# Second attention of a macaron block: scores from row tiles, and the order of a group's phases

## The reference

```python
def _L1_attn_ref(data, W_qkv, b_qkv, W_out, b_out):
    N, L, D_IN, H, HD, D_OUT = (4, 256, 128, 16, 64, 128)
    DIM = H * HD
    n, l = (data.shape[0], data.shape[1])
    qkv = data @ W_qkv + b_qkv
    q = qkv[:, :, :DIM].reshape(n, l, H, HD)
    k = qkv[:, :, DIM:2 * DIM].reshape(n, l, H, HD)
    v = qkv[:, :, 2 * DIM:].reshape(n, l, H, HD)
    scores = jnp.einsum('nqhd,nkhd->nhqk', q, k)
    attention = jax.nn.softmax(scores / jnp.sqrt(jnp.float32(HD)), axis=3)
    out = jnp.einsum('nhql,nlhd->nqhd', attention, v).reshape(n, l, DIM)
    return out @ W_out + b_out
```

## Time and profile before

| | |
|---|---|
| three executions | 3102.01, 3099.66, 3099.52 us; median 3099.66 |
| the profiled execution | 3094.67 us |
| its span, first to last instruction | 3092.9 us |
| mean granted TensorE clock | 0.961 of full speed |
| busy in the span | TensorE 91%, VectorE 67%, GpSimd 57%, ScalarE 56% |
| the second attention | from about 1850 to 2880 us of the span |

### The profile page before, as it was taken

One profiled execution on the slowest core, in us unless ns is written; L12 is line 12 of the kernel. 1 busy time (PEld: TensorE's weight loads), 2 busy tenths in 40 slices (PEclk: granted clock), 3 DMA queues, 4 the chain that ended last, 5 costly groups with the idle time before them and its releaser, 6 DMA issues. The chain is left out here.

```text
span 3092.9 us, 48070 instructions
## 1 busy us (share of the span) xinstructions
PE 2824.9 (91%) x16692; PEld 1889.5 (61%) x16692; DVE 2087.2 (67%) x4491; ACT 1733.2 (56%) x3334; POOL 1751.1 (57%) x1540
## 2 busy tenths in 40 slices
PE   7999999999999999989993869999999999999376
PEld 6995555555555555548882765656556565565276
DVE  5667777777677777766777437676776777767542
ACT  5665767677676767676761434444544544444033
POOL 0005989898888989881100764554554545455067
PEclk9999999999999999989995889999999999999678
DMA  3003434343343334320001436444444445443033
GB/s 99 1 15 91 102 84 103 84 96 89 85 97 91 89 86 96 85 67 11 15 22 61 94 64 137 111 94 102 110 107 103 110 95 116 92 103 90 28 78 53
DMA packets 182946, 251.89 MB, mean 81 GB/s; under 512 B 36084, under 2 KB 75569, under 8 KB 182193
## 3 DMA queue, kind: packets, MB, share of 16 engines
q1 hardware_dynamic: 168624, 238.09, 32.8%
q0 software_dynamic: 14080, 10.73, 2.5%
HBM read 31.34 MB, written 14.57 MB: 15 GB/s over the span
## 5 line engine op out<-in xcount | busy, mean ns | idle before, releaser
L1919 POOL TENSOR_TENSOR arena<-arena 128x512 f32<-128x512 f32 x1152 | 1445.0, 1282 | 675.9 <-ACT arena L1277 570.0
L1277 ACT ACTIVATE arena<-psum 128x512 f32<-128x512 f32 x1536 | 843.2, 600 | 523.4 <-PE psum L872 519.1
L1555 DVE TENSOR_REDUCE top<-psum 128x1 f32<-128x512 f32 x1536 | 958.4, 672 | 68.8 <-PE psum L872 67.8
L872 PE MATMUL psum<-stack 96*128 96x512 f32 (+3 forms) x3072 | 949.9, 431 | 19.2 <-ACT arena L1277 9.1
L872 PEld LDWEIGHTS psum<-stack 96*128 96x128 f32 (+3 forms) x3072 | 521.5, 190 | 320.5 <-issue 158.3
L923 PE MATMUL psum<-arena,values 128*32 128x512 f32 (+1 forms) x3072 | 495.9, 600 | 12.7 <-ACT arena L1277 12.7
L923 PEld LDWEIGHTS psum<-arena,values 128*32 128x32 f32 (+1 forms) x3072 | 129.7, 119 | 286.7 <-issue 228.1
L1888 POOL TENSOR_SCALAR rstd<-mv 128x4 f32<-128x4 f32 x56 | 13.1, 235 | 450.2 <-DVE mv L1417 448.9
L1586 DVE RECIPROCAL psum<-psum 128x128 f32<-128x128 f32 x256 | 243.6, 955 | 34.4 <-PE psum L955 34.4
L883 PE MATMUL psum<-halves 64*128 64x512 f32 x1536 | 214.9, 409 | 3.8 <-DVE top L1555 3.8
L757 PE MATMUL psum<-stack 128*128 128x512 f32 x768 | 211.5, 411 | 0.1
(11 more groups left out here) (176 smaller groups left out, 3528.1 us busy)
## 6 DMA issues: line engine op xcount, KB each, us to landing
stack<-halves SPq DMA_DIRECT2D x768, 128.0 KB, 2.3
stack<-halves SPq DMA_DIRECT2D x384, 256.0 KB, 4.7
tokens<-xn SPq DMA_DIRECT2D x16, 256.0 KB, 2.4
arena<-in_wg SPq DMA_DIRECT2D x16, 256.0 KB, 3.0
arena<-in_wu SPq DMA_DIRECT2D x16, 256.0 KB, 3.5
arena<-in_wd SPq DMA_DIRECT2D x16, 256.0 KB, 3.0
wqkv<-in_w_qkv SPq DMA_DIRECT2D x2, 1536.0 KB, 8.9
X<-in_x SPq DMA_DIRECT2D x8, 256.0 KB, 4.6
```

The costliest lines, as they stand in the source:

```text
L872: ins = T_.matmul(bk, st[0:k, side, slot + h, cols], st[0:k, 1 - side, slot + h, :], start=r == 0, stop=r == len(PARTS[l]) - 1)
L1277: S_.activation(prob[l][tile % N_PROB][:, h, :], psum[:, bank[key], :], ACT.Exp, scale=scale).then_inc(released[bank[key]], 1)
L1555: give(V_.reduce_max(top[i][:, column:column + 1], psum[:, bank[key], :], AX.X), key)
L1919: ins = G_.tensor_tensor(to[:, h, :], old[:, h, :], prob[l][tile % N_PROB][:, h, :], ALU.add)
```

## The change

The second attention no longer uses stacks of halves. `probabilities` takes its scores from `halves` through the same function as `maxima`: `both_heads` gets the keys and a list of rounds, three products and a fourth round of 64 rows, which multiplies rows of ones with rows of minus the maximum (`ones_rows`, `top_rows`, in the memory of the stacks; zero apart from two rows for each head). The halves are kept for four groups instead of two (`split`), in `halves` and two parts of the stacks. All copies of the halves into stacks go; the maxima are copied by four DMAs instead of two. The queries' scores of a pair are now one tile of queries of both heads, as before, but a pair is issued at a time instead of two (`AT_ONCE` goes). q, k, v and top of the second attention take their banks from the ring of the scores. `weigh` does its four tiles in `last` and none in `probs`; probabilities have eight buffers instead of five. The table of times of the second attention is new. The first attention keeps its way.

```diff
-    dict(project=(-0.11, 0.61), maxima=(0.90, 1.11), maxima2=(0.95, 1.29), rows=(1.90, 1.90), probs=(2.33, 3.28),
-         last=(3.19, 3.46), mix=(3.91, 4.52), out=(4.59, 4.83), ahead=(-2.58, -0.89), route=(4.85, 6.56),
-         ranks=(6.66, 7.31), keep=(7.88, 7.88)))
+    dict(rows=(1.82, 1.82), queries=(0.75, 0.75), keys=(0.80, 0.80), values=(1.01, 1.01), maxima=(1.04, 1.48),
+         probs=(3.03, 3.47), last=(3.43, 4.05), sums=(4.38, 4.38), mix=(4.38, 4.83), out=(4.93, 4.97),
+         ahead=(-1.52, 0.45), route=(5.03, 10.53), ranks=(9.80, 10.86), keep=(10.00, 10.00)))
...
-            self.once(self.other, (w, l, n))
+            self.once(self.products if l else self.other, (w, l, n))
...
-        self.once(self.other, ("top", l, n))
+        self.once(self.products if l else self.other, ("top", l, n))
...
+                if l == 0:
+                    self.once(self.products, ("prob", l, n, kt, h))
+                elif h == 0:
+                    for head in range(HEADS[l]):
+                        self.once(self.products, ("prob", l, n, kt, head))
+                yield
...
+        split = (halves, halves + [stack[i][:, 1, :, :] for i in range(2)])
+        top_rows = [stack[i][:, 0, 0, :] for i in range(N_STACK)]
+        ones_rows = [stack[i][:, 0, 1, 0:P] for i in range(N_STACK)]
...
-        N_PROB = 5
+        N_PROB = (5, 8)
...
+            def both_heads(keys, rounds):
+
+                banks = [place(key) for key in keys]
+                for r, (weights, moving) in enumerate(rounds):
                     for h, (bk, done) in enumerate(banks):
                         rows_h = slice(64 * h, 64 * (h + 1))
-                        ins = T_.matmul(bk, hv[rows_h, q, pair * P:(pair + 1) * P], hv[rows_h, k, :],
-                                        start=r == 0, stop=r == 2, tile_position=(64 * h, 0))
-                        if r == 2:
+                        ins = T_.matmul(bk, weights[rows_h], moving[rows_h], start=r == 0, stop=r == len(rounds) - 1,
+                                        tile_position=(64 * h, 0))
+                        if r == len(rounds) - 1:
                             ins.then_inc(done, 1)
...
+                        elif h == 0:
+                            both_heads([("prob", l, n, kt, head) for head in range(HEADS[l])],
+                                       [(hv[:, k, cols], hv[:, q, :]) for q, k in ((QH, KH), (QL, KH), (QH, KL))]
+                                       + [(ones_rows[n % N_STACK], top_rows[n % N_STACK])])
                         yield
-                    if kt == 2:
+                    if kt == 2 and l == 0:
                         weigh(l, n, 0)
                         weigh(l, n, 1)
                         yield
...
             def last_tiles(l, n):
-                weigh(l, n, 2)
-                weigh(l, n, 3)
+                for kt in range(0 if l else 2, TILES_B):
+                    weigh(l, n, kt)
                 yield
...
-                    if n >= 2:
-                        act.wait_ge(*all_stacked(l, n - 2))
-                        if l:
-                            act.wait_ge(*written(("score", l, n - 2, HEADS[l] * TILES_B - 1)))
+                    if n >= len(split[l]):
+                        act.wait_ge(*halves_used(l, n - len(split[l])))
...
             def project(l, n):
-                s, hv, st, width = n % N_STACK, halves[n % 2], stack[n % N_STACK], WIDTH[l]
+                if l:
+                    return
...
+                    if l:
+                        for h in range(HEADS[l]):
+                            Y_.dma_start(
+                                top_rows[s][64 * h + r:64 * h + r + 1, :].rearrange("a (t q) -> a t q", t=TILES_B).bitcast(fp32),
+                                part[h * TILES_B:(h + 1) * TILES_B, :].bitcast(fp32)).then_inc(max_rows[s], 16)
```

More of the change, by code:

```diff
@@ L117, in queue @@
             start, end = WHEN[l][part]
-            part = dict(ranks="route", maxima2="maxima").get(part, part)
+            part = dict(ranks="route", queries="project", keys="project", values="project").get(part, part)
             stream(part, numbers, calls, steps, at + n + start, at + n + end)
@@ L298, in last @@
     def last(self, l, n):
+        if l:
+            self.mixed.take(("o", l, n))
         yield
@@ L648, in free, with all_stacked, halves_used @@
             return (released[bank[key]], nth[key]) if nth[key] else None
[L650 to L653, removed]
+        def all_stacked(n):
+            return stacked[n % N_STACK], 16 * 3 * HEADS[0] * (n // N_STACK + 1)
+        def halves_used(l, n):
+            return written(("prob", 1, n, TILES_B - 1, HEADS[1] - 1)) if l else all_stacked(n)
         def all_max_rows(l, n):
@@ L730, in idle_tile @@
         def idle_tile(slot):
-            tile = max(t for t in range(N_GROUPS * TILES_B) if t % N_PROB == slot)
+            tile = max(t for t in range(N_GROUPS * TILES_B) if t % N_PROB[0] == slot)
             return tile_weighed(0, *divmod(tile, TILES_B)), tile_summed(0, *divmod(tile, TILES_B))
@@ L867, in project, with product @@
                 yield
[L869 to L876, removed]
-                hv = halves[n % 2]
-                banks = [place(("score", 1, n, 2 * pair + h)) for h in range(2)]
-                for r, (q, k) in enumerate(((QH, KH), (QL, KH), (QH, KL))):
+            def product(bk, st, side, h, cols, k):
+                return T_.matmul(bk, st[0:k, side, h, cols], st[0:k, 1 - side, h, :], start=True, stop=True)
+            def both_heads(keys, rounds):
+                banks = [place(key) for key in keys]
+                for r, (weights, moving) in enumerate(rounds):
                     for h, (bk, done) in enumerate(banks):
                         rows_h = slice(64 * h, 64 * (h + 1))
-                        ins = T_.matmul(bk, hv[rows_h, q, pair * P:(pair + 1) * P], hv[rows_h, k, :],
-                                        start=r == 0, stop=r == 2, tile_position=(64 * h, 0))
-                        if r == 2:
+                        ins = T_.matmul(bk, weights[rows_h], moving[rows_h], start=r == 0, stop=r == len(rounds) - 1,
+                                        tile_position=(64 * h, 0))
+                        if r == len(rounds) - 1:
                             ins.then_inc(done, 1)
@@ L901, in maxima @@
                     for i in range(HEADS[l] * TILES_B):
-                        if i % AT_ONCE == 0:
-                            for pair in range(i // 2, (i + AT_ONCE) // 2):
-                                both_heads(n, pair)
+                        qt, h = divmod(i, HEADS[l])
+                        if h == 0:
+                            cols = slice(qt * P, (qt + 1) * P)
+                            both_heads([("score", l, n, i + head) for head in range(HEADS[l])],
+                                       [(hv[:, q, cols], hv[:, k, :]) for q, k in ((QH, KH), (QL, KH), (QH, KL))])
                         yield
@@ L962, in mix @@
                     return
-                columns = [inverse[l][n % 2][:, t * P:(t + 1) * P] for t in range(TILES_B)]
+                columns = [inverse[n % 2][:, t * P:(t + 1) * P] for t in range(TILES_B)]
                 yield
```

108 lines of the change are left out of this document (59 added, 49 removed).

## The result

The changed kernel takes 3107.27 us (median of 11 runs, 3103.72 to 3112.72), the kernel before 3102.01 on the same chip (11 runs, 3098.2 to 3107.1): ratio 1.002, 95% interval 1.0011 to 1.003. So it is slower by about 5 us, just short of the 0.2% that I took as the bound of "same"; forecast was 3154, in a range from 3090 that holds the result. The profiled execution of after took 3106.33 us (span 3104.5, clock 0.960), that of before 3094.67: the profiles lie 11.6 apart, since the execution profiled of before is a quick one.

The account below looks back on a forecast made before the run. TensorE was taken to bound the kernel, busy 123.86 of 127.2 us a batch. Groups +49, seam -2, batches +12, start -7, drain +2 on 3094.67 gave 3149; 5 more for the median gave 3154, range 3090 to 3190.

Parts of the forecast that it names:

- Removing the copies: Stack copies and their DMAs in the second attention: TensorE doesn't wait for them, so removal is worth 0 by itself.
- Fewer changes of shape: TensorE's tile shapes: three changes a group instead of six, 0.21 us each, minus 0.63 us a group.
- The row tiles: Probability scores as 16 row-tile pairs instead of 16 full matmuls: 0.23 us a round, minus 0.06 us a group.
- The bank chain: Each probability pair (P) waits for a bank the previous one filled: P to P 2.0 us, plus 1.2 a group.
- Rival 1: The banks don't bind: a bank returns in 1.6 us, group 13.9 us, about 3080 in the median; chance 0.20.
- The group: One plain group of the second attention: 15.1 us against 14.3, plus 0.8 (0.81 in the sum).
- The seam: Next group's first probability pair waits for q's bank, 2.75 us after q: plus 0.24 a group, output groups excepted.
- Batch work: Normalisation, moments and router work inserted in each batch: 5 us instead of 3.3, plus 1.7 per batch.
- five such insertions: Normalisation, moments and router ranks delaying ScalarE or VectorE: about 1 us each, bounded by 0 and 1.63.
- Ends: Start and drain of the second attention's pipeline: minus 7 us at the start, plus 2 in the drain.
- Rival 2: Gain and loss cancel: P to P 1.8 us, batch waits gone, group 14.5, 3098 to 3105; chance 0.08.
- Rival 3: VectorE makes it slower still, 3200 us, if q's low half starts later than 1.9 us after q; chance 0.12.

Follow-up runs that it names:

- e5: Transposition of the maxima moved between the first two probability pairs of the next group, against the seven-bank kernel e2: 3113.96 us, ratio 1.0012.
- e9: Store of a finished batch (keep) moved from 10.00 to 10.90, behind the router's last step, against e5: 3066.14 us, ratio 0.9855.
- e7: Table of times of the kernel before (phases mixed, ten shape changes a group) put into the seven-bank kernel e2: 3141.95 us, ratio 1.0103.
- e2: Seven banks instead of five in the second attention's ring, weighed values included, against the changed kernel: 3035.87 us, ratio 0.9769 to the kernel before.

## Why the prediction was right or wrong

**Removing the copies, 0: right, as far as waits show it** (no run takes the copies away and leaves the rest). No wait for a DMA stands in TensorE's waits of the second attention, before or after, and the DMAs fell from 251.89 to 151.32 MB. In one variant a copy of the maxima was waited for, through SP's order (e5), which after doesn't have.

**Fewer changes of shape, 0.21 each: right, slightly low.** 0.24 (e5), 0.23 (e9), 0.27 (e7). The trace agrees with the rule of the Trainium skill, "TensorEngine Tiling (Array Packing)", Key Properties, that a change of tiling mode drains the array and that another tile of the same mode doesn't. Its warning, in Restrictions and Gotchas, of PSUM pressure under row tiling is what decided the case: with seven banks the change is worth -2.3%, with its five +0.2%.

**The row tiles, 0.23 a round: right,** 0.91 for four where nothing waits (e2).

**The bank chain, P to P 2.0: right, link by link;** one of the three steps is 1.94. 1.26 to the exponential, 0.60, 0.14. Rival 1 needed 1.6 and is refuted for this kernel; it describes e2.

**The group, +0.81: the sum was right in kind, measured +0.52.** Three terms were too high and one too low. P to P came to 5.94 instead of 6.0 (-0.06: one of three starts 1.94 after the last). The last P and S to the sums took 1.81 instead of 1.93 (-0.12: the last P and S ran with 0.06 less each than the links I had added up). Column phase 4.44 instead of 4.41 (+0.03). The seam took 2.61 instead of 2.75 (-0.13: ScalarE began q's high half 0.07 sooner and VectorE followed 0.07 sooner than the links I copied from other rows). Together -0.28, times 61 that is 17 us.

**Batch work, +1.7 a batch: the step that failed.** With the seam's 0.24 off for the output group that is +1.5; measured -2.9, and the difference of 4.4 makes 31 us over seven batches. The sentence was "I put five such insertions at about 1 us each, bounded by 0 and by the 1.63 of the one measured: 5 us instead of 3.3". There were three, of 0.54, 0.55 and 0.64, 1.7 in all: two pairs behind a normalisation on ScalarE (one of them shown above), and one in the group of the router's ranks, which waits for a maximum. The working's fault was to take the insertion's length as the upper bound. In a step of 2.0 us ScalarE has two exponentials of 0.60 and is idle for the rest; an insertion fills that first and delays only by what is left, here 1.64 - 1.04 = 0.6, measured 0.5 to 0.55. That is 3.3 of the 4.4.

The other 1.1 are two smaller faults beside it. The 3.3 us that it took for the waits before are TensorE's idle time; from start to start, against the same places of a plain group, the waits before add up to 3.8 (1.5 for the exponential and 1.5 for the transposition of the earlier trace rows, 0.5, 0.2 and 0.1 behind them). And not one group in eight escapes the seam's wait but four:

```profile
...
2070.62 0.50 PE L771 MATMUL psum<-x_cols_high,qkv_high 128*128 128x512 f32 x1
...
2071.43 0.60 PE L776 MATMUL psum<-cst,xn 128*128 128x128 f32 x4
...
2073.47 0.96 PE L893 MATMUL psum<-halves 64*128 64x512 f32 x6
...
```

With a transposition of normalised rows (0.35 us) between q and P0 the distance is 2.85, which is the 2.40 of seven banks plus that transposition and its neighbours: the low half of q is ready by then. So it is in the two groups with a transposition, in the one with the router's matmuls and in the output group, 0.85 a batch instead of 0.24. TensorE's own batch work is the same in both orders: 7.1 us for the outputs, 0.7 for the transpositions, 0.8 for the router. The account closes: 1.7 - 3.8 - 0.85 = -2.9.

**Ends.** Fill -5.9 to the first score pair of group 2, -6.5 to its transposition of maxima, forecast -7; drain +3.6, forecast +2. Both are near, the drain by some luck: the parts that the prediction lists for it, one after the other and with two column phases, make 7.8 + 9.0 + 7.7 + 3.4 = 27.9 us, 5.8 over 22.1, and how it came to +2 isn't said. So of the 42 us between the forecast's +54 and the profiles' +12, the plain groups have 17 and the batches 31; ends and first batch give some 5 back. Between the medians the difference is 6 us smaller still, by the draw of the two profiled executions.

**Rival 2, that gain and loss cancel (0.08), comes nearest to what was measured**, by half of its own mechanism: it asked for P to P at 1.8, which didn't come, and for the batch waits gone, which did in good part. **Rival 3** (VectorE) didn't: q's low half starts 1.72 after q, under its point of 1.9.

**What I said the profile would show.** Bank waits and the seam: there. Fewer DMAs: there. Batches near 134 us: 128.4. A busy share of 92%: it is 96.7% (124.11 of 128.4), and this was an error of reading: a wait of up to 0.16 us lies wholly within the modelled end of the matmul before it (0.39, where the next starts after 0.23), and a longer one loses that much. Of "a group under 14.3 or P 1.6 apart" neither came.

## What to carry to other kernels

A pair of row tiles here fills two banks at once, so before pairing matmuls write down the bank turn: fill, time to the reader, reader, release, against the array's own time between two fills of that bank; here 2.0 us against 1.6, and one more bank in the ring gave 1.9%. Grouping matmuls by tile shape pays (0.25 us a change; ten changes down to three gave 3.3%), but only with banks enough for it, and the ring that the phased order needs did harm in the mixed one. Work put on an engine in a bank chain costs its length less the engine's idle time in the step, not its length. And judge TensorE's waits by distances from start to start, as busy shares and wait lists hide waits of one or two tenths that come hundreds of times.

## What the runs showed of the hardware that was not expected

A change of shape cost 0.23 to 0.27 us in three kernels, more than the 0.21 derived from the kernel before. Around each wait of TensorE of some 4 us, once a batch, the granted clock was at its lower level for 3.4 to 6.8 us (e5), so that e5 lost 49 us with waits of 32. The exponential shortens a good deal less than its columns: 594 to 381 ns for half of them, so about 170 ns of it don't depend on the size.
